# Rows of x loaded as 32x32 squares, normalised by ScalarE and turned by VectorE, in a decoder layer's recurrence

## The reference

```python
# 1, recurrence (the part that the change rewrites)
xn = layernorm(x)
z  = sigmoid(einsum('bsd,ndk->bsnk', xn, Wz) + bz)      # 4 groups of 128 features
h~ = einsum('bsd,ndk->bsnk', xn, Wh) + bh
h[t] = (1 - z[t]) * h[t-1] + z[t] * h~[t]               # associative scan over the tokens
x  = x + sigmoid(h @ Wg + bg) * h
# 2, attention of 16 heads over 77 context rows
x  = x + attention(layernorm(x), ctx) @ Wo + bo
# 3, two of four experts for each token
x  = x + sum of weight_k * expert_k(layernorm(x)),  expert = norm(relu(norm(x W1 + b1)) W2 + b2)
```

## Time and profile before

| | |
|---|---|
| median of three runs | 1167.13 us (1164.18 to 1169.15) |
| the profiled execution | 1170.26 us, of which its span is 1168.5 us |
| TensorE (PE) busy | 1108.3 us, 95% of the span, 6017 products |
| VectorE (DVE) busy | 910.5 us, 78% |
| ScalarE (ACT) busy | 722.2 us, 62% |
| GpSimd (POOL) busy | 393.4 us, 34% |
| granted TensorE clock, mean | 0.991 |

### The profile page before, as it was taken

The page is one execution under the profiler, slowest core; times in us unless marked ns, Lnnn a source line. Parts: engine busy times, 40 slices in busy tenths (PEclk is TensorE's granted clock), DMA queues, the critical chain, the costliest instruction groups (busy, mean ns, idle before and its releaser), DMA issues.

```text
span 1168.5 us, 24237 instructions
## 1 busy us (share of the span) xinstructions
PE 1108.3 (95%) x6017; PEld 905.0 (77%) x6018; DVE 910.5 (78%) x2172; ACT 722.2 (62%) x2148; POOL 393.4 (34%) x328
## 2 busy tenths in 40 slices
PE   6999999999989999999999888999999999999993
PEld 5888888888877787777777666777888888888882
DVE  6888888887874778878878877877777777777774
ACT  5223332233377777768676644866787787877873
POOL 3000000000034433545536364445534434443432
PEclk9999999999999999999999998999999999999998
DMA  8544545445340133143143377786555454444543
GB/s 261 163 149 159 190 148 173 151 163 207 126 147 1 57 89 111 56 124 100 46 145 90 128 206 219 201 249 152 94 85 81 81 85 80 86 81 81 88 63 40
DMA packets 95316, 144.76 MB, mean 124 GB/s; under 512 B 20864, under 2 KB 37428, under 8 KB 94607
## 3 DMA queue, kind: packets, MB, share of 16 engines
q1 hardware_dynamic: 77338, 106.83, 28.8%
q0 software_dynamic: 17216, 35.73, 17.4%
q10 hardware_dynamic: 693, 1.36, 0.4%
HBM read 82.69 MB, written 64.76 MB: 126 GB/s over the span
## 4 chain that ended last, share of the span: by engine, by line
PE 72%; DVE 9%; issue 7%; DMA 6%; ACT 3%; POOL 2%; DVEq 0%; POOLq 0%; ACTq 0%; SPq 0%
PE banks L1126 27%; PE banks L716 17%; PE banks L928 7%; PE banks L781 6%; DMA out<-rows,scatter_rows 4%; PE banks L893 3%; PE banks L906 3%; PE banks L1154 2%; PE banks L1138 2%; ACT rows L1335 2%; DVE operands L1615 2%; PE banks L917 1%; PE banks L754 1%; DVE rows L1917 1%; ACT operands L1218 1%
## 5 line engine op out<-in xcount | busy, mean ns | idle before, releaser
L1126 PE MATMUL banks<-operands 128*128 x1608 | 390.5, 398 | 9.2 <-ACT operands L1218 5.0
L1126 PEld LDWEIGHTS banks<-operands 128*128 128x128 f32 x1608 | 299.5, 190 | 73.9 <-issue 14.2
L716 PE MATMUL banks<-operands 128*128 128x512 f32 (+2 forms) x1224 | 290.1, 393 | 3.6 <-DVE operands L1615 3.6
L716 PEld LDWEIGHTS banks<-operands 128*128 128x128 f32 (+1 forms) x1224 | 226.1, 192 | 48.3 <-DVE operands L1615 3.7
L1218 ACT ACTIVATE operands<-banks 128x512 fp32r<-128x512 f32 (+1 forms) x232 | 137.6, 602 | 63.4 <-PE banks L807 34.2
L1615 DVE TENSOR_TENSOR operands<-banks,operands 128x512 fp32r<-128x512 f32 (+1 forms) x232 | 156.7, 683 | 15.6 <-ACT operands L1218 12.2
L1335 ACT ACTIVATE rows<-banks,score_shift 128x77 f32<-128x77 f32 x512 | 158.4, 337 | 11.2 <-DVE score_shift L1839 10.9
L2686 POOL DMA_INDIRECT out<-rows,scatter_rows x67 | 106.4, 1588 | 155.3 <-DVE rows L2419 109.7
L1218 ACT ACTIVATE operands<-rows 128x512 fp32r<-128x512 f32 (+2 forms) x77 | 54.0, 710 | 163.6 <-DVE rows L1686 139.4
L1540 ACT ACTIVATE banks<-banks,param_cols 128x128 f32<-128x128 f32 x268 | 99.2, 431 | 82.2 <-PE banks L1154 75.6
L2357 DVE BATCH_NORM_STATS2 moe_stats<-banks 128x6 f32<-128x512 f32 x134 | 93.2, 696 | 37.5 <-PE banks L1126 31.5
(11 more groups left out here) (191 smaller groups left out, 1603.1 us busy)
## 6 DMA issues: line engine op xcount, KB each, us to landing
expert_parts<-operands SPq DMA_DIRECT2D x32, 512.0 KB, 3.0
operands<-expert_parts SPq DMA_DIRECT2D x8, 2048.0 KB, 11.4
rows<-in_x SPq DMA_DIRECT2D x8, 1024.0 KB, 5.5
rows<-in_L_ffn_W SPq DMA_DIRECT2D x32, 256.0 KB, 3.6
x_rows<-rows SPq DMA_DIRECT2D x8, 1024.0 KB, 4.3
rows<-x_rows SPq DMA_DIRECT2D x8, 1024.0 KB, 6.2
xf_rows<-rows SPq DMA_DIRECT2D x32, 256.0 KB
out<-rows SPq DMA_DIRECT2D x32, 256.0 KB
```

Of the source, the lines that this page charges most:

```text
L716: last = nc.tensor.matmul(dst, stationary(a, k), moving(b, k), start=(t == 0 and k == 0), stop=(t == len(terms) - 1 and k == n_k - 1))
L1126: last = nc.tensor.matmul(dst, stationary[:, a, k, :], weights[:, w, bass.ds(e, 1), a2, k, :].rearrange("p e f -> p (e f)"), start=False, ...
```

## The change

- The rows of x for chunks 1 to 7 are loaded a second time, as 32x32 squares (`load_squares`, four DMAs of 32 partitions for each chunk), into `xn`. ScalarE normalises them there (`normalise_x`: for each 128 tokens four instructions of 128x128, with scale and bias by partition), and VectorE turns the squares (`turn_x`, one STREAM_TRANSPOSE of 128x512 for each 128 tokens) into `xT_rows`. TensorE's transposes of these chunks go, and so does VectorE's normalising.
- The scale and the bias stand by token; the squares need them by partition of the square. GpSimd makes the product of mean and factor, TensorE spreads both with four products (`spread_scales`, 128x8 each) into the bank of the gates, and VectorE copies the 32 columns out.
- Features are in another order in a turned square, so the rows of Wz and Wh are loaded in that order, by 16 DMAs of 32 partitions each instead of 4, and chunk 0, which TensorE still transposes, is normalised into that order.
- 1 - z is made by ScalarE into a tile of its own (`za_left`) and not by VectorE.
- The new tiles stand where `kblk` was. So the keys go to DRAM first, `kblk` is cleared by GpSimd in two pieces at the end of the recurrence, and SP places the keys in the last chunk (`place_keys`).
- Several semaphores are merged.

```diff
+        Q = nc.alloc_sbuf_tensor_at("recurrence_rows", [P, 77 * KB_ // 4], F32, offset=r_base + 48 * 1024)
...
 # SP
             for raw, name, loaded in ((raw_wz, "L0_attn_Wz", wz_in), (raw_wh, "L0_attn_Wh", wh_in)):
                 for n in range(KC):
-                    sp.dma_start(raw[:, :, n * P:(n + 1) * P],
-                                 io[name][n].rearrange("(k p) f -> p k f", p=P)).then_inc(loaded, 16)
+                    for q in range(KC):
+                        sp.dma_start(raw[q * SQ:(q + 1) * SQ, :, n * P:(n + 1) * P],
+                                     io[name][n][q * P:(q + 1) * P, :].rearrange("(k r) f -> r k f", r=SQ)).then_inc(
+                            loaded, 16)
...
+            def load_squares(c):
+                src = x_sq[c] if isinstance(c, int) else x_sq[bass.ds(c, 1)].rearrange("c r b f -> (c r) b f")
+                for q in range(KC):
+                    sp.dma_start(xn[q * SQ:(q + 1) * SQ].rearrange("p j (b f) -> p (j b) f", f=P),
+                                 src[:, :, q * P:(q + 1) * P]).then_inc(xp_in, 16)
+            def place_keys():
+                sp.wait_ge(pool_step, 2)
+                for hl in range(HPG):
+                    rows = slice(hl * DH, (hl + 1) * DH)
+                    for a in (HI, LO):
+                        sp.dma_start(kblk[rows, a, :, :, hl * SK:(hl + 1) * SK].bitcast(F32),
+                                     kT_d[rows, a]).then_inc(k_placed, 16)
...
+                    if n == 3 and c_squares:
+                        need_alone(sp, x_turned, 4 * (c + 1), passed)
+                        load_squares(c + 2)
+                    if n == 3 and isinstance(c, int) and c == NCH - 1:
+                        place_keys()
...
 # TensorE
+            def spread_scales(c):
+                pe.wait_ge(ln1_rstd, rstd_steps(c))
+                need(pe, gate_ready, 4 * (c - 1))
+                for b in range(P // SQ):
+                    last = nc.tensor.matmul(g_bank[0][:, b * 2 * TPC:(b + 1) * 2 * TPC],
+                                            spread[:, b].rearrange("p q r -> p (q r)"), sc1_cols, start=True, stop=True)
+                last.then_inc(sc_done, 1)
...
+                    if m == (1 if back else 2) and not (isinstance(c, int) and c == NCH - 1):
+                        spread_scales(c + 1)
...
-                if ahead:
-                    transpose_x(c + 1, (0, 1))
-                else:
+                if not ahead:
...
 # ScalarE
+            def x_hi(c, ks):
+                if ks[0] == 0:
+                    act.wait_ge(h_done, 4 * c)
+                    act.wait_ge(x_turned, 4 * c)
+                for k in ks:
+                    hi_part(xnT[:, HI, k, :], xT_rows[:, k, :]).then_inc(xnT_hi, 1)
+            def normalise_x(c, js):
+                for j in js:
+                    if j == 0:
+                        act.wait_ge(xp_in, 16 * KC * c)
+                        act.wait_ge(sc_in, c)
+                    for b in range(P // SQ):
+                        square = xn[:, j, b * P:(b + 1) * P]
+                        last = nc.scalar.activation(square, square, ACT.Identity, scale=sc_sq[:, b, 0, j:j + 1],
+                                                    bias=sc_sq[:, b, 1, j:j + 1])
+                    last.then_inc(xn_ready, 1)
...
                     nc.scalar.activation(za[:, m % 2, :], z_bank[m % 2], ACT.Sigmoid,
                                          bias=pcol[:, ROW_BZ + m:ROW_BZ + m + 1]).then_inc(z_ready, 1)
+                    act.wait_ge(z_ready, n + 1)
+                    nc.scalar.activation(za_left[:, m % 2, :], za[:, m % 2, :], ACT.Identity, scale=-1.0,
+                                         bias=ones[:, 0:1]).then_inc(a_ready, 1)
+                    if not last:
+                        normalise_x(c + 1, ((), (), (), (0, 1, 2, 3))[m] if first else ((), (0, 1), (2,), (3,))[m])
...
 # VectorE
-            def ln1_apply(c):
-                dve.wait_ge(ln1_rstd, c + 1)
...
+            def turn_x(c, js):
+                for j in js:
+                    dve.wait_ge(xn_ready, 4 * c + j + 1)
+                    V.transpose(xT_rows[:, :, j * P:(j + 1) * P].rearrange("p k (b r) -> p b k r", r=SQ),
+                                xn[:, j].rearrange("p (b k r) -> p b k r", b=KC, k=KC)).then_inc(x_turned, 1)
...
-                V.tensor_scalar(za[:, m % 2, :], za[:, m % 2, :], -1.0, 1.0, ALU.mult, ALU.add).then_inc(a_ready, 1)
...
+                    if ahead and m == (2 if first else 1):
+                        dve.wait_ge(sc_done, c + 1)
+                        V.tensor_copy(sc_sq_cols, g_bank[0][:, 0:CH // SQ * 2]).then_inc(sc_in, 1)
                     if m == (2 if first else 1):
                         split_piece_lo(c, 0)
...
+                    if ahead:
+                        turn_x(c + 1, ((), (), (), ())[m] if first else ((), (), (0, 1), (2,))[m])
                 h_lo(c, KC - 1)
+                if ahead:
+                    turn_x(c + 1, (0, 1, 2, 3) if first else (3,))
                 split_piece_lo(c, 1)
...
-                if ahead >= 2:
-                    ln1_apply(c + 2)
...
 # GpSimd
+                G.tensor_tensor(sc1[:, 0, :], ve1[:, :], half[:, 0:TPC], ALU.pow).then_inc(ln1_rstd, 1)
+                pool.wait_ge(ln1_rstd, rstd_steps(c) - 1)
+                G.tensor_tensor(sc1[:, 1, :], sc1[:, 1, :], sc1[:, 0, :], ALU.mult).then_inc(ln1_rstd, 1)
...
+            pool.wait_ge(xnT_lo, 4 * (NCH - 1))
+            G.memset(r_at(48, int(15.25 * KB_)).bitcast(F32), 0.0)
+            pool.wait_ge(h_ready, KC * NCH)
+            G.memset(r_at(63.25, 4 * KB_).bitcast(F32), 0.0).then_inc(pool_step, 1)
```

More of the change, by code:

```diff
@@ L498, in a_chunk @@
             def a_chunk(c, first):
+                c_squares = not isinstance(c, int) or c < NCH - 2
                 for n in range(4):
@@ L744, in values_of, with transpose_first @@
                         lambda a, k: wv[:, a, k, :]).then_inc(v_done, 1)
-            def transpose_x(c, ks=range(KC)):
+            def transpose_first(ks):
                 for k in ks:
-                    g = t_group(c) + k
-                    need(pe, a_t_read, g - 1)
+                    need(pe, a_t_read, k - 1)
                     for j in range(TPC):
                         if k == 0:
-                            pe.wait_ge(xn_ready, 4 * c + j + 1)
+                            pe.wait_ge(xn_ready, j + 1)
                         last = nc.tensor.transpose(t_bank[k % 2][:, j * P:(j + 1) * P],
@@ L826, in gates @@
                     gate_terms(c, m, (KC - 1,)).then_inc(g_done, 1)
-                if ahead:
-                    transpose_x(c + 1, (2, 3))
-                else:
+                if not ahead:
                     x1_to_features(0, -1, (2, 3))
@@ L1240, in _ @@
             weight_hi(wv, raw_wv, wv_in, 32)
[L1241 to L1243 removed]
+            weight_hi(wz, raw_wz, wz_in, 256)
+            x_hi_first((0, 1))
+            weight_hi(wh, raw_wh, wh_in, 256)
             act.wait_ge(pcol_ready, 1)
@@ L1648, in ln1_stats @@
+                if not (isinstance(c, int) and c < 2):
+                    need_alone(dve, sc_in, c - 1, passed)
                 for j in range(TPC):
-                    V.bn_aggr(mv1[:, j, :], st1[:, j, :]).then_inc(ln1_aggr, 1)
-                dve.wait_ge(ln1_aggr, 4 * (c + 1))
-                need(dve, ln1_rstd, c)
+                    V.bn_aggr(mv1[:, j, :], st1[:, j, :]).then_inc(ln1_stat, 1)
+                dve.wait_ge(ln1_stat, 8 * (c + 1))
+                if not (isinstance(c, int) and c == 0):
+                    V.tensor_scalar(sc1[:, 1, :], mv1[:, :, 0], -1.0, None, ALU.mult)
@@ L1652, in ln1_stats, with first_rows @@
                 V.tensor_scalar_add(ve1[:, :], mv1[:, :, 1], EPS).then_inc(ln1_eps, 1)
-            def ln1_apply(c):
-                dve.wait_ge(ln1_rstd, c + 1)
-                need(dve, a_t_done, t_group(c - 1) + 4 if not (isinstance(c, int) and c == 0) else 0)
+            def first_rows():
+                dve.wait_ge(ln1_rstd, rstd_steps(0))
                 for j in range(TPC):
-                    V.tensor_scalar(xn[:, j, :], xr(c, j), mv1[:, j, 0:1], rs1[:, j:j + 1],
-                                    ALU.subtract, ALU.mult).then_inc(xn_ready, 1)
@@ L1662, in x_lo, with x_lo_first @@
+            def x_lo_first(ks):
+                for k in ks:
+                    dve.wait_ge(xnT_hi, k + 1)
+                    lo_part(xnT[:, LO, k, :], t_bank[k % 2], xnT[:, HI, k, :]).then_inc(a_t_read, 1)
+            def x_lo(c, ks):
                 for k in ks:
                     dve.wait_ge(xnT_hi, 4 * c + k + 1)
-                    lo_part(xnT[:, LO, k, :], t_bank[k % 2], xnT[:, HI, k, :]).then_inc(a_t_read, 1)
+                    lo_part(xnT[:, LO, k, :], xT_rows[:, k, :], xnT[:, HI, k, :]).then_inc(xnT_lo, 1)
@@ L1747, in a_chunk @@
                     if first and m == 1:
-                        dve.wait_ge(k_placed, 16 * 2 * HPG)
```

(11 more changed lines are left out.)

133 lines of the change are left out of this document (70 added, 63 removed).

## The result

The changed kernel takes 1209.05 us (median of four runs, 1206.5 to 1213.15), the kernel before 1168.14 in the same session: 1.036 times as long, 95% interval 1.0325 to 1.0398. The forecast was 1196 with a range to 1208. The profiled execution took 1208.59 us, its span 1206.7, against 1170.26 and 1168.5.

The account below looks back on a forecast made before the run. TensorE and VectorE were taken to bound a chunk almost equally. Loop +18.0, chunk 0 +7.4, last chunk -1.0, start +1.0 and clock +4.0 gave +29.4 on 1170.3, 1199.7, stated as 1196 us for the median; range 1178 to 1208.

Parts of the forecast that it names:

- The loop's wait: Chunks 1 to 6: VectorE's lo part waits behind ScalarE's eight affines, TensorE idles before the gates; +18.0 us for six.
- The clock: TensorE's clock halves after idle stretches of 3.4 us in seven chunks: 1.3 us a chunk, 0 to 9, taken as +4.
- Rival (2): Recurrence: the clock falls in each chunk and affines cost 0.43 us; +38, 1205 us; chance 0.10.
- The last chunk: No transposes or affines there, VectorE earlier, and the eight transposes of L807 no longer wait: -1.0 us.
- Chunk 0: First chunk: TensorE waits for the spread factors, sixteen affines delay ScalarE's hi parts, then turns follow: +7.4 us.
- The start: Weight loading: sixteen issues replace four for each of two weights; bounds 0 and +3, taken as +1.0 us.
- Sizes: Prices of new operations: affines 0.37 us each (0.20 to 0.43), turns 681 ns, four spreading products 0.5 us (0.2 to 1.05).
- Key placing: Stage's end: covered by gate products and first queries; priced at nothing, 3 us at most if the landing is slow.
- GpSimd's product in the loop: Loop chunks: GpSimd's extra product has half a chunk to spare, so no cost.
- the second reading of x: Loop chunks: four issues, 1.9 us, before one expert load needed only after the last gate; hidden, no cost.
- Rival (3): Wait before gate products: TensorE stays the bound, freed transposes pay 1.2 us a loop chunk; about -10, 1157; chance 0.07.

Follow-up runs that it names:

- e_warm: Changed kernel plus constant-weight products that keep TensorE busy at the waits before the gates and chunk 0's spreading products: 1197.45 us, 1.0255 of the kernel before.
- e_order: Changed kernel with only ScalarE's order altered, the expert piece's hi part before the affines: 1183.83 us, 1.0135 of the kernel before.
- e_memset: Changed kernel with GpSimd's clearing held until VectorE has normalised the next stage's first four rows: 1202.38 us, 1.0312 of the kernel before.
- e_best2: Changed kernel with hi part, chunk 0, clearing and gate-side hi parts of x reordered, Wh split later, squares loaded behind the store: 1164.76 us, 0.9985 of before.
- e_chunk0: Changed kernel with only chunk 0 reordered (earlier statistics, affines spread out, later hi parts of x): 1199.45 us, 1.0292 of the kernel before.
- e_flip: Kernel before with only 1 - z moved from VectorE to ScalarE: 1163.47 us, 0.9960 of before; second time 1163.74, 0.9975.

## Why the prediction was wrong

The direction, the place and the mechanism of the loop's wait were right; of the 41 us, 29 were foreseen. What failed is the term of the clock, 4 us for some 12, and next to it the sign of the last chunk.

- **The loop's wait: right.** The walk said that the lo part of the expert piece starts 18.4 us into a chunk (192.55 - 174.15), the third lo part of h comes at 27.05, the gates start at 27.75; in the chunk from 200.07 it is 18.59, 27.11 and 27.81. Forecast for a chunk 39.5; with the clock held 39.41 to 39.44 (e_warm). Six chunks without the clock cost 16.6 us (235.8 - 219.2), said 18.0: chunk 6 is shorter. e_order shows the cause.
- **The clock: the step that failed.** "0 to 9 us in all; I take 4." The size of one fall was right, 1.3 a chunk: chunks 2, 4, 5 and 6 lost 1.25 to 1.4. How often it falls was not: in five chunks of six, and chunk 1 lost 2.4, chunk 0 2.65. That is 10.4 us in chunks 0 to 6 of the two traces; the timed medians differ by 11.6. With the fall that e_warm leaves in chunk 0, estimated at 7.36 - 5.73 = 1.6 us, it is some 12 instead of 4. These 8 us alone bring the forecast to 1204; with the 3.2 of the last chunk it is 1207, the edge of the range. The row at 792.05 had shown a fall after a shorter wait (2.24 us) than the 3.4 forecast here, so no row spoke for counting fewer than half of the waits. Rival (2) had a fall in each chunk with a chance of 0.10; its other half, affines at 0.43 us, did not come (0.39). The Trainium skill ("TensorE: Matmul & The Clock Gate", Part 1) says that an idle array drops to half its clock until it has been busy; the trace agrees in five chunks of six and shows no fall in chunk 3 at the same wait.
- **The last chunk: -1.0 was wrong, it is +2.2.** The clearing that the change moved to GpSimd stood beside VectorE's normalising and held it for 3.1 us. With the clearing later the last chunk takes 36.71 us, 0.8 less than before (e_memset), so the rest of the term was nearly right. I had asked whether the keys come late, which they don't, and not what the clearing itself collides with. The Trainium skill has the rule ("SBUF — State Buffer", section on who interferes with whom): GpSimd and VectorE lock one pair of ports for a whole instruction when VectorE's runs in a two-port mode, as TENSOR_SCALAR may; one of two SBUF inputs is held only by a GpSimd instruction that reads SBUF. The traces agree with both halves: 5.03 for 1.91 us, and 0.69, 0.75 and 1.29 unchanged.
- **Chunk 0: +7.4 said, +12.1 measured.** The miss is the clock again: 2.65 us that e_warm took away and the 1.6 that it left. Without them +7.8 remain, so the walk itself was within half a us. The spreading products start 19.92 us into the chunk (50.61 - 30.69); said 19.66 (48.9 - 29.24).
- **The start: +1.0 said, +1.45 measured**; in the other traces with the same issue order at the start the first z comes at 30.3 to 34.0, so +3 was no upper bound (e_best2, where Wh is split later, has 28.81). ScalarE waited for Wh 1.67 us.
- **Sizes:** affines 0.39 each (0.37 said), turns 695 ns (681), the four spreading products 0.95 us, twice the 0.5 taken, since each is two instructions; all within the bounds. Key placing and GpSimd's product in the loop cost nothing that the traces show, as said, and neither does the second reading of x in the changed kernel. Once chunk 0 is reordered its place in SP's queue does count: the forecast asked only about the load behind it, and the store behind it made chunk 1 1.9 us longer (e_chunk0).

Rival (3), that the freed transposes pay, was rejected for the right reason: it needs the wait gone. With the wait gone (e_best2) it holds in part and in the trace alone, 0.4 us a chunk against e_flip where 1.2 were named, and not in the timed runs.

What stays open: why the clock kept up in chunk 3 (in one run chunk 6, in two the last chunk) after such an idle stretch, and why e_best2's 5.6 us at the end of the stage are some 2.5 in the timed medians; the expert stage's own spread of 7.6 us could hide the difference.

## What to carry to other kernels

When work moves to an engine with time to spare, ask what already stands in its order for the busy engine: here one 0.6 us hi part behind 3.2 us of affines cost 25 us in six chunks, 7.75 of them by the clock, and exchanging the two gave them back. Price every new wait of TensorE twice, once for itself and once for the clock behind it, and count that second price at every wait unless a trace shows that it does not come. Try the parts of a change one by one: here the smallest of them held all of the gain that the timed runs show.
